# Gated delta-rule attention with two routed experts: value tiles turned through DRAM and in 32 x 32 blocks instead of by matmuls

## The chip, the cores and the metric

One Trainium2 chip, of which the kernel uses one core. The metric is the device time of one execution in microseconds (us), the median of several runs. Beside it stands one execution taken by the hardware profiler, with its own time.

## What is computed

A sequence of 2048 tokens with 512 features is normalised, and goes through two branches whose product is added to the input. The first branch is a recurrent attention with 16 value heads and 8 key heads (two value heads share a key head); the second is a feed-forward layer with the two experts that the router picks.

```python
xn = layernorm(x)
q, k, v = split(silu(causal_conv(xn @ W_qkv)))     # 8 + 8 + 16 heads of 128
q, k = l2norm(q) * 128 ** -0.5, l2norm(k)          # each repeated for two value heads
beta, g = sigmoid(xn @ W_b), -exp(A_log) * softplus(xn @ W_a + dt_bias)
def step(S, (q, k, v, g, beta)):                   # for each token and value head
    S = S * exp(g)
    S = S + outer(k, (v - k @ S) * beta)
    return S, q @ S
o = scan(step)
s = (o * rsqrt(mean(o * o) + eps) * norm_weight * silu(xn @ W_z)) @ W_out
y = x + s * silu(experts(xn))                      # two of eight experts
```

## The kernel before

The recurrence is computed by chunks of 128 tokens. A block is 512 tokens (4 chunks, `CPS`) of one key head with its two value heads (`REP`); there are 32 blocks (`NU`), four to a key head. All engines have their programs written by hand, one function each (`tensor` for PE, `scalar` for ACT, `vector` for DVE, `gpsimd` for POOL, `sync` for the DMA queue of SP), and each engine runs its instructions in the order in which they are written. They wait for each other by counting semaphores (`S_`). In each of these functions `attention_step(st)` is called for st = 2 to 34 at the most, and works on up to four blocks at once: it projects and convolves block st (`now`) and parts of block st + 1 (`ahead`), prepares block st - 1 (`turned`) and runs the chain of the recurrence over block st - 2 (`chain`).

A value tile goes this way. PE projects 512 tokens of one value head (`project` with kind v0 or v1) into a PSUM bank, ACT multiplies it by the first tap (`tap`), DVE adds the other three (`convolve`, three instructions of 128 x 512), and ACT writes the SiLU into `vS`, with features on the partitions and tokens along them. The chain needs tokens on the partitions. So `turn_v(st, half)` on PE turns two chunks of two heads by four matmuls with the identity, into a PSUM bank; it is called twice a step, behind `chain_out(st - 2, 1)` and behind `chain_out(st - 2, 2)`. `put_v(st, half)` on ACT then copies the turned tiles to `v_tok`, each token multiplied by the length of its key (`roots`). `chain_R` on DVE reads `v_tok` one step later.

Each of the four links i of the chain is: `chain_keys` (PE, keys and queries times the state S; waits for S), `chain_R` (DVE), `chain_solve` (PE), `chain_U` (ACT, copies U out of PSUM), `chain_state` and `chain_out` (PE, both read U), `chain_S` (DVE, the new S). PE fills the time between the links with projections. At the end of a step stand on PE `chain_state(3)`, `chain_out(3)`, `pair_matrices`, `join_y64`, then in the next step `chain_keys(0)` and `turn_q`; on DVE `chain_S(3)`, in each fourth block a clearing of S (`zero_state`), and `convolve(st, "v0")`. `turn_q` writes the bank from which `convolve(st, "v0")` reads, and so waits for its last instruction:

```python
def turn_q(st):
    ...
        pe.wait_ge(S_["conv_v0"], CONV * b)
```

A second loop runs beside the chain: small triangular inverses. 32 x 32 pieces of `CP` go to DRAM (`a_dram`), come back spread over the partitions (`A_in`), POOL eliminates, the result goes to DRAM (`v_dram`) and comes back into `VT`; DVE turns its diagonal blocks (`diagonal`, line 1400), and PE joins them (`join_y32`, line 511). The queue of SP also fetches decays (`E`, `decb`) and weights (`w_raw`), in the order of its program. After the attention come the experts (`up`, `down`), during which the results are turned by way of `og_x` and `og_y` (DVE, 32 x 32 blocks), and the output projection.

Of the kernel before, what the change touches and what calls it, by code (L numbers as in the profile page):

```python
# [6 lines left out]
P = 128  # L7
T, D = 2048, 512
KEY_HEADS, HEADS, HD = 8, 16, 128
KW = 4  # L10
# [65 lines left out]
rows_out eg0 eg1 dec0 dec1 begin0 begin1 a_out a_in v_out vt_in  # L76
xT smallT ab_turned sums score_parts scores_sum rows_turned
proj_k proj_q proj_v0 proj_v1 z_proj k_turned q_turned v_turned pair_kq keys queries solved state_add out_add lev_y32 lev_z32 lev_y64 lev_z64
sw_hi xn_hi ab_T ab_in exp_steps exp_sum rows
tap_k tap_q tap_v0 tap_v1 act_k act_q act_v0 act_v1 carry_k carry_q carry_v0 carry_v1 z_gate q_sq k_rem v_tok U squares y32 z32 y64 inv w_hi  # L80
softplus_steps router_steps stats var shift xn xn_lo beta softplus router rows_zero
conv_k conv_q conv_v0 conv_v1 nk nk_eps nk_beta c_neg c_rem q_eps CP E V_diag S_zero R S ms og w_lo_kq
# [8 lines left out]
def build(nc, x, small_w, group_w, conv_w, dt_bias, a_log, norm_w, w_out, w1, b1, w2, b2, const, where, og_dram, out):  # L91
# [5 lines left out]
    with top:  # L97
# [9 lines left out]
        ogT_dram = nc.dram_tensor("ogT_dram", (NT, P, HEADS, P), f32, kind="Internal").ap()  # L107
        v_dram = nc.dram_tensor("v_dram", (2, NPROB, B32, B32), f32, kind="Internal").ap()
# [28 lines left out]
        vS = alloc(att, "vS", [REP, SB])  # L137
# [54 lines left out]
        v_tok = alloc(p2b, "v_tok", [2, CPS, REP * HD])  # L192
# [57 lines left out]
        TQ_BANK, TK_BANK, TV_BANK = WORK_B, WORK_C, (WORK_C, WORK_B)  # L250
# [65 lines left out]
        CONV = 3  # L316
        SOLVES = B32 - 1
# [21 lines left out]
        def tensor(pe):  # L339
# [79 lines left out]
            def project_v0(st):  # L419
                if is_block(st - 1):  # L420
                    pe.wait_ge(S_["v_tok"], 2 * st)
                else:
                    pe.wait_ge(S_["conv_k"], CONV * 2)
                project(st, "v0")
# [57 lines left out]
            def turn_k(st):  # L482
                b = st - 1
                pe.wait_ge(S_["v_tok"], 2 * b + 1)
# [3 lines left out]

            def turn_v(st, half):
                b = st - 1  # L490
                pe.wait_ge(S_["act_v0"], b + 1)
                pe.wait_ge(S_["act_v1"], b + 1)
                if half:
                    pe.wait_ge(S_["z_gate"], CPS * b + 3)
                elif is_block(st):
                    pe.wait_ge(S_["CP"], CPS * (st + 1))
                elif b:
                    pe.wait_ge(S_["k_rem"], b)
                for i in range(2):
                    c = 2 * half + i  # L500
                    for h in range(REP):
                        r = pe.transpose(TV_BANK[half][:, (REP * i + h) * P:(REP * i + h + 1) * P], vS[:, h, c * P:(c + 1) * P], C["ident"])  # L502
# [1694 lines left out]
```

## Time and profile before

| | |
|---|---|
| median of 3 runs | 2063.14 us (2057.46 to 2063.60) |
| the profiled execution: its time | 2060.95 us |
| its span, first to last instruction | 2059.2 us |
| mean granted TensorE clock | 0.989 of full speed |
| busy: PE, DVE, ACT, POOL | 97%, 65%, 44%, 41% |
| attention, its steady steps | from about 140 to 1190 us |

The profile is of one execution. Busy is the time in which an engine executes, as a share of the span; it is a mean over stages with different limits. "Idle before" names the engine whose work ended last before an instruction could start. Matmuls overlap each other, so the distance between the starts of two groups tells better than their durations how long PE was taken. In the timeline a row can stand for several like instructions (x2, x4). PE, DVE, ACT, POOL are the engines; SPq and ACTq are DMA issues by SP and ACT.

### The profile page before, as it was taken

The numbers are of one execution on the slowest core, as the hardware profiler recorded it, in microseconds if no ns is written. First come the engines' busy times: TensorE is split into PE (matmuls) and PEld (weight loads), VectorE is DVE, ScalarE is ACT, GpSimd is POOL, SyncE is SP. The second block draws the span as 40 slices with busy tenths as digits, with TensorE's granted clock in tenths as the row PEclk, the third lists the DMA queues.
The fourth block names the chain that finished last, engine by engine and source line by source line (L and its number), as shares of the span: only waits on it lengthen the run. The fifth ranks groups of instructions, "written<-read, shape, count | busy, mean of one in ns | idle before, by whom it ended". The sixth has DMA issues, their size and how long they took to land.

```text
span 2059.2 us, 39550 instructions
## 1 busy us (share of the span) xinstructions
PE 1997.2 (97%) x13730; PEld 1705.4 (83%) x13730; DVE 1337.3 (65%) x3097; ACT 911.0 (44%) x2525; POOL 836.8 (41%) x2123
## 2 busy tenths in 40 slices
PE   5789999999999999999999999999999999999999
PEld 3578888888888888888888888888888888887887
DVE  6768887778787777887786445555555444447442
ACT  4465555555556565655554532222333233224221
POOL 2456576666666665757665411000111110111111
PEclk8899999999999999999999999999999999999999
DMA  4234444454336444444444223433334534303441
GB/s 131 47 74 81 102 87 96 82 94 83 93 84 106 82 98 92 86 92 84 97 80 85 84 82 72 92 78 76 83 80 84 123 82 103 72 21 123 154 149 66
DMA packets 388022, 184.25 MB, mean 89 GB/s; under 512 B 249456, under 2 KB 369136, under 8 KB 385776
## 3 DMA queue, kind: packets, MB, share of 16 engines
q1 hardware_dynamic: 354640, 177.73, 37.9%
q10 hardware_dynamic: 33184, 4.01, 1.3%
q8 instruction: 110, 1.80, 0.4%
q14 instruction: 88, 0.72, 0.1%
HBM read 135.26 MB, written 46.40 MB: 88 GB/s over the span
## 4 chain that ended last, share of the span: by engine, by line
PE 75%; issue 10%; DVE 6%; DMA 3%; POOL 3%; ACT 3%; SPq 1%; POOLq 0%; ACTq 0%; DVEq 0%
PE bank L333 18%; PE bank L335 18%; PE bank L334 18%; PE bank L565 3%; PE bank L574 2%; PE bank L548 2%; DMA VT<-v_dram 2%; PE bank L468 2%; PE bank L556 2%; PE bank L584 2%; PE bank L527 2%; PE bank L533 2%; POOL y_out L1825 1%; PE bank L502 1%; DVE cvx_k L1340 1%
## 5 line engine op out<-in xcount | busy, mean ns | idle before, releaser
L1771 POOL TENSOR_TENSOR prod<-A_in,V 128x60 f32<-128x60 f32 (+24 forms) x992 | 304.0, 306 | 270.6 <-DMA A_in<-a_dram 200.2
L1773 POOL TENSOR_TENSOR V<-V,prod 128x60 f32<-128x60 f32 (+24 forms) x992 | 311.6, 314 | 77.7
L1098 ACT ACTIVATE hid<-bank,bias 128x512 f32<-128x512 f32 x128 | 88.4, 691 | 455.0 <-PE bank L335 453.2
L1815 POOL TENSOR_TENSOR ffn_w_lo<-ffn_raw,ffn_w_hi 128x1024 fp32r<-128x1024 f32 x32 | 78.0, 2439 | 468.6 <-ACT ffn_w_hi L1088 464.7
L1563 DVE TENSOR_TENSOR h_lo<-hid,h_hi 128x512 fp32r<-128x512 f32 x128 | 91.1, 712 | 266.0 <-ACT h_hi L1105 266.0
L1577 DVE SCALAR_TENSOR_TENSOR gate_acc<-bank,rw,gate_acc 128x512 f32<-128x512 f32 x240 | 177.4, 749 | 58.8 <-PE bank L335 58.8
L333 PE MATMUL bank<-ffn_w_hi,h_hi 128*128 128x512 f32 x512 | 199.3, 389 | 1.3 <-DVE h_lo L1563 1.0
L333 PE MATMUL bank<-xn_hi,ffn_w_hi 128*128 128x512 f32 x512 | 200.3, 391 | 0.0
L335 PE MATMUL bank<-xn_hi,ffn_w_lo 128*128 128x512 f32 x512 | 199.3, 389 | 0.0
L334 PE MATMUL bank<-xn_lo,ffn_w_hi 128*128 128x512 f32 x512 | 199.2, 389 | 0.0
L334 PE MATMUL bank<-ffn_w_lo,h_hi 128*128 128x512 f32 x512 | 199.2, 389 | 0.0
L335 PE MATMUL bank<-ffn_w_hi,h_lo 128*128 128x512 f32 x512 | 199.2, 389 | 0.0
L1442 DVE SCALAR_TENSOR_TENSOR S<-S,total,bank 128x128 f32<-128x128 f32 x256 | 77.5, 344 | 139.9 <-PE bank L574 138.6
L333 PE MATMUL bank<-w_hi_z,xn_hi 128*128 128x256 f32 x512 | 154.1, 301 | 7.5 <-DVE cvx_v L1340 4.8
L1340 DVE SCALAR_TENSOR_TENSOR cvx_v<-bank,taps,cvx_v 128x512 f32<-128x512 f32 x192 | 143.0, 745 | 7.7 <-ACT cvx_v L874 3.1
L334 PE MATMUL bank<-w_lo_z,xn_hi 128*128 128x256 f32 x512 | 143.4, 280 | 0.0
L335 PE MATMUL bank<-w_hi_z,xn_lo 128*128 128x256 f32 x512 | 143.4, 280 | 0.0
L333 PEld LDWEIGHTS bank<-ffn_w_hi,h_hi 128*128 128x128 f32 x512 | 96.1, 188 | 21.8 <-issue 2.1
L335 PEld LDWEIGHTS bank<-ffn_w_hi,h_lo 128*128 128x128 f32 x512 | 96.2, 188 | 20.1
L334 PEld LDWEIGHTS bank<-xn_lo,ffn_w_hi 128*128 128x128 f32 x512 | 96.3, 188 | 19.5
L335 PEld LDWEIGHTS bank<-xn_hi,ffn_w_lo 128*128 128x128 f32 x512 | 96.0, 188 | 19.9
L333 PEld LDWEIGHTS bank<-xn_hi,ffn_w_hi 128*128 128x128 f32 x512 | 96.1, 188 | 19.7
(222 smaller groups left out, 5151.2 us busy)
## 6 DMA issues: line engine op xcount, KB each, us to landing
E<-eg_dram SPq DMA_DIRECT2D x64, 256.0 KB, 7.6
A_in<-a_dram SPq DMA_DIRECT2D x32, 512.0 KB, 4.0
decb<-dec_dram SPq DMA_DIRECT2D x128, 128.0 KB, 4.2
og_dram<-og SPq DMA_DIRECT2D x64, 256.0 KB, 2.2
ffn_raw<-w SPq DMA_DIRECT2D x32, 512.0 KB, 4.0
og_x<-og_dram SPq DMA_DIRECT2D x256, 64.0 KB, 2.6
ogT_dram<-og_y SPq DMA_DIRECT2D x64, 256.0 KB, 2.4
og_in<-ogT_dram SPq DMA_DIRECT2D x16, 1024.0 KB, 5.3
```

The costliest lines, as they stand in the source:

```text
L333: pe.matmul(ps, lh, rh, start=first, stop=False)
L334: pe.matmul(ps, lh, rl, start=False, stop=False)
L335: return pe.matmul(ps, ll, rh, start=False, stop=last)
L565: r = pe.matmul(bank[K_BANK][:, (REP + h) * HD:(REP + h + 1) * HD], VT[:, b % 2, REP * i + h, :], R[:, h, :], start=True, stop=True)
L1098: act.activation(hid[:, i % 2, :], bank[i % 4][:, :], ACT.Gelu_apprx_tanh, bias=bias1[:, k, f * NF + ft:f * NF + ft + 1]).then_inc(S_["gel ...
L1340: dve.scalar_tensor_tensor(cv[:, at], P_BANK[kind][:, :], taps[:, 4 * gr + n, j:j + 1], cv[:, at], MUL, ADD).then_inc(S_[f"conv_{kind}"], 1)
L1442: r = dve.scalar_tensor_tensor(S[:, h, :], S[:, h, :], total[:, cg, h0 + h:h0 + h + 1], bank[K_BANK][:, h * HD:(h + 1) * HD], MUL, ADD)
L1563: dve.tensor_tensor(h_lo[:, hb, ft, :], hid[:, i % 2, :], h_hi[:, hb, ft, :].bitcast(f32), SUB).then_inc(S_["h_lo"], 1)
L1577: dve.scalar_tensor_tensor(gate_acc[:, t, :], bank[4 + c][:, :], rw[:, k, t:t + 1], gate_acc[:, t, :], MUL, ADD).then_inc(S_["acc"], 1)
L1771: pool.tensor_tensor(prod[:, 0:m, 0:n], column, V[:, vb, 0:m, j:j + 1].to_broadcast([P, m, n]), MUL).then_inc(S_["product"], 1)
L1773: pool.tensor_tensor(V[:, vb, 0:m, j + 1:B32], V[:, vb, 0:m, j + 1:B32], prod[:, 0:m, 0:n], ADD).then_inc(S_["solve_step"], 1)
L1815: pool.tensor_tensor(fw[m, "lo", n % 2][:, :], raw[:, i % 2, :], fw[m, "hi", n % 2][:, :].bitcast(f32), SUB).then_inc(S_["ffn_lo"], 1)
```

## The change

The eight matmuls per block that turn the value tiles are gone from PE, with the PSUM banks that they used. In their place:

- `silu` writes the two heads side by side by chunks into `vS`, and `store_v` on ACT stores `vS` to DRAM (`vs_dram`) with one DMA of 512 KB, 128 rows of 4 KB, right behind `silu(v1)`, ahead of `chain_U(st - 2, 1)`.
- `load_v` on SP loads it back with four DMAs of 128 KB into `v_x`, in pieces of 32 values (128 bytes), behind the two decay loads in the second half of the step. After this load each 32 x 32 block is in the place where it has to be, but not yet turned.
- `turn_v` on DVE turns the blocks, in two instructions of 128 x 512 (two chunks of two heads each), behind `chain_S(st - 2, 3)` and ahead of `convolve(st, "v0")`, and writes `v_tok`, of which there is now one instead of two.
- `put_v` on ACT multiplies `v_tok` in place by the key lengths, both halves at the end of the step behind `put_y64`.
- Some waits follow: `project_v0` on PE waits for the third z gate instead of for `put_v`; `turn_k` takes over the wait that `turn_v` had; the four semaphores `carry_...` become one.

```diff
--- before
+++ after
...
@@ -105,6 +105,7 @@
         ogT_dram = nc.dram_tensor("ogT_dram", (NT, P, HEADS, P), f32, kind="Internal").ap()
+        vs_dram = nc.dram_tensor("vs_dram", (B32, NQD, REP * SB), f32, kind="Internal").ap()
         v_dram = nc.dram_tensor("v_dram", (2, NPROB, B32, B32), f32, kind="Internal").ap()
@@ -134,7 +135,7 @@
         q_sq = alloc(att, "q_sq", [4, CPS])
-        vS = alloc(att, "vS", [REP, SB])
+        vS = alloc(att, "vS", [CPS, REP, P])
         neg_inv = alloc(att, "neg_inv", [NT, HEADS])
@@ -189,7 +190,8 @@
         Y64 = alloc(p2b, "Y64", [NCH, 2 * B32])
-        v_tok = alloc(p2b, "v_tok", [2, CPS, REP * HD])
+        v_tok = alloc(p2b, "v_tok", [CPS, REP, HD])
+        v_x = alloc(p2b, "v_x", [NQD * REP * CPS, B32])
         z_gate = alloc(p2b, "z_gate", [2, CPS, REP * HD])
@@ -247,7 +249,7 @@
         KQ_BANK = (WORK_C, WORK_C)
-        TQ_BANK, TK_BANK, TV_BANK = WORK_B, WORK_C, (WORK_C, WORK_B)
+        TQ_BANK, TK_BANK = WORK_B, WORK_C
 
@@ -314,6 +316,7 @@
         CONV = 3
+        X_SET = 16 + 16 * NQD
         SOLVES = B32 - 1
@@ -418,7 +421,7 @@
                 if is_block(st - 1):
-                    pe.wait_ge(S_["v_tok"], 2 * st)
+                    pe.wait_ge(S_["z_gate"], CPS * (st - 1) + 3)
                 else:
@@ -481,26 +484,13 @@
                 b = st - 1
-                pe.wait_ge(S_["v_tok"], 2 * b + 1)
+                if is_block(st):
+                    pe.wait_ge(S_["CP"], CPS * (st + 1))
+                else:
+                    pe.wait_ge(S_["k_rem"], b)
                 for c in range(CPS):
                     i = pe.transpose(TK_BANK[:, c * P:(c + 1) * P], kqT[:, b % KQ_LIFE, c, 0, :], C["ident"])
                 i.then_inc(S_["k_turned"], 1)
-
-            def turn_v(st, half):
-                b = st - 1
-                pe.wait_ge(S_["act_v0"], b + 1)
-                pe.wait_ge(S_["act_v1"], b + 1)
-                if half:
-                    pe.wait_ge(S_["z_gate"], CPS * b + 3)
-                elif is_block(st):
-                    pe.wait_ge(S_["CP"], CPS * (st + 1))
-                elif b:
-                    pe.wait_ge(S_["k_rem"], b)
-                for i in range(2):
-                    c = 2 * half + i
-                    for h in range(REP):
-                        r = pe.transpose(TV_BANK[half][:, (REP * i + h) * P:(REP * i + h + 1) * P], vS[:, h, c * P:(c + 1) * P], C["ident"])
-                r.then_inc(S_["v_turned"], 1)
 
@@ -616,8 +606,6 @@
                     chain_out(st - 2, 1)
-                if turned:
-                    turn_v(st, 0)
 
@@ -631,7 +619,6 @@
                 if turned:
-                    turn_v(st, 1)
                     turn_k(st)
...
@@ -858,19 +841,23 @@
+            carries = 0
+                nonlocal carries
+                carries += 1
-                    act.copy(cv[:, 0:KW - 1], C["zero"][:, 0:KW - 1]).then_inc(S_[f"carry_{kind}"], 1)
+                    act.copy(cv[:, 0:KW - 1], C["zero"][:, 0:KW - 1]).then_inc(S_["carry"], 1)
-                    act.copy(cv[:, 0:KW - 1], cv[:, SB:SB + KW - 1]).then_inc(S_[f"carry_{kind}"], 1)
+                    act.copy(cv[:, 0:KW - 1], cv[:, SB:SB + KW - 1]).then_inc(S_["carry"], 1)
-                act.wait_ge(S_[f"carry_{kind}"], b + 1)
+                act.wait_ge(S_["carry"], carries)
@@ -886,8 +873,9 @@
                     if b:
-                        act.wait_ge(S_["v_turned"], 2 * b)
-                    dst = vS[:, int(kind[1]), :]
+                        act.wait_ge(S_["v_x"], X_SET * b)
+                    dst = vS[:, :, int(kind[1]), :]
+                    src = src.rearrange("p (c t) -> p c t", c=CPS)
                 act.activation(dst, src, ACT.Silu).then_inc(S_[f"act_{kind}"], 1)
@@ -923,12 +911,19 @@
                     act.wait_ge(S_["k_len"], b + 1)
-                if b >= 2:
-                    act.wait_ge(S_["R"], CPS * (b - 1))
                 for i in range(2):
                     c = 2 * half + i
-                    r = act.mul(v_tok[:, b % 2, c, :], TV_BANK[half][:, i * REP * HD:(i + 1) * REP * HD], roots[:, b % 4, c:c + 1])
+                    r = act.mul(v_tok[:, c, :, :], v_tok[:, c, :, :], roots[:, b % 4, c:c + 1])
                 r.then_inc(S_["v_tok"], 1)
+
+            def store_v(b):
+                act.wait_ge(S_["act_v0"], b + 1)
+                act.wait_ge(S_["act_v1"], b + 1)
+                if b:
+                    act.wait_ge(S_["v_turned"], 2 * b)
+                else:
+                    act.wait_ge(S_["xT"], 14)
+                act.dma_start(vs_dram.rearrange("i b t -> b i t"), vS[:, :, :, :].rearrange("p c h t -> p (c h t)")).then_inc(S_["v_x"], 16)
 
@@ -1020,6 +1015,7 @@
                     silu(st - 1, "v1")
+                    store_v(st - 1)
                 if chain:
@@ -1030,8 +1026,6 @@
                     mean_squares(st - 2, 1)
-                if turned:
-                    put_v(st, 0)
 
@@ -1044,7 +1038,6 @@
                 if turned:
-                    put_v(st, 1)
                     put_k(st)
@@ -1073,6 +1066,8 @@
                     put_y64(st - 1)
+                    put_v(st, 0)
+                    put_v(st, 1)
 
...
@@ -1400,6 +1396,15 @@
 
+            def turn_v(b):
+                dve.wait_ge(S_["v_x"], X_SET * (b + 1))
+                if b:
+                    dve.wait_ge(S_["R"], CPS * b)
+                for half in range(2):
+                    src = v_x[:, :, :].rearrange("p (b c h) j -> p c h b j", b=NQD, h=REP)[:, 2 * half:2 * half + 2, :, :, :].rearrange("p c h b j -> p (c h) b j")
+                    dst = v_tok[:, 2 * half:2 * half + 2, :, :].rearrange("p c h (b j) -> p (c h) b j", b=NQD)
+                    dve.transpose(dst, src).then_inc(S_["v_turned"], 1)
+
             def split_weights(n):
@@ -1417,7 +1422,7 @@
                     r = dve.scalar_tensor_tensor(R[:, h, :], bank[K_BANK][:, h * HD:(h + 1) * HD], decay[:, cg, h0 + h:h0 + h + 1],
-                                                 v_tok[:, b % 2, i, h * HD:(h + 1) * HD], MUL, SUB)
+                                                 v_tok[:, i, h, :], MUL, SUB)
                 r.then_inc(S_["R"], 1)
@@ -1547,6 +1552,8 @@
                     chain_S(st - 2, 3)
+                if turned:
+                    turn_v(st - 1)
                 if now:
...
@@ -1926,6 +1934,13 @@
 
+            def load_v(b):
+                sp.wait_ge(S_["v_x"], X_SET * b + 16)
+                for q in range(NQD):
+                    r = slice(q * B32, (q + 1) * B32)
+                    src = vs_dram.rearrange("i b (m t) -> i (b m) t", t=P)[:, :, r]
+                    sp.dma_start(v_x[r, :, :], src).then_inc(S_["v_x"], 16)
+
             def store(p):
@@ -1971,6 +1986,8 @@
                 next_decay(3)
+                if turned:
+                    load_v(st - 1)
                 if now and st % NSB == 1 and group + 1 < KEY_HEADS:
...
```

The order of instructions on three engines, at one place each; names are those of tiles, L is the line in the kernel's own file, x2 a count of like instructions.

On DVE, from the end of a step that clears no state, over its last state update into the next step, before:

```order
L1466 SCALAR_TENSOR_TENSOR og<-bank,roots,z_gate 128x128 x4
L1344 SCALAR_TENSOR_TENSOR E<-E,cst 128x256 x2
L1442 SCALAR_TENSOR_TENSOR S<-S,total,bank 128x128 x2
L1340 SCALAR_TENSOR_TENSOR cvx_v<-bank,taps,cvx_v 128x512 x3
L1363 SCALAR_TENSOR_TENSOR CP,norms<-bank,cst 128x128 x2
```

and after the change:

```order
L1471 SCALAR_TENSOR_TENSOR og<-bank,roots,z_gate 128x128 x4
L1340 SCALAR_TENSOR_TENSOR E<-E,cst 128x256 x2
L1447 SCALAR_TENSOR_TENSOR S<-S,total,bank 128x128 x2
L1406 STREAM_TRANSPOSE v_tok<-v_x 128x512 x2
L1336 SCALAR_TENSOR_TENSOR cvx_v<-bank,taps,cvx_v 128x512 x3
L1359 SCALAR_TENSOR_TENSOR CP,norms<-bank,cst 128x128 x2
```

Two transposes have come between the state update and the convolution whose end `turn_q` waits for.

On PE, behind the second link of the chain (state, out, then keys of the third link), before:

```order
L335 MATMUL bank<-w_hi_z,xn_lo 128x256
L574 MATMUL bank<-U,k_rem 128x128 x2
L584 MATMUL bank<-U,CP 128x128 x2
L502 MATMUL bank<-cst,vS 128x128 x4
L548 MATMUL bank<-S,kqT 128x256
L556 MATMUL bank<-S,qd 128x128 x2
```

and after the change:

```order
L338 MATMUL bank<-w_hi_z,xn_lo 128x256
L564 MATMUL bank<-U,k_rem 128x128 x2
L574 MATMUL bank<-U,CP 128x128 x2
L538 MATMUL bank<-S,kqT 128x256
L546 MATMUL bank<-S,qd 128x128 x2
```

The keys of the third link now stand directly behind the second link's output.

On ACT, in the first half of a step, before:

```order
L984 DMA a_dram<-CP 32x8x32 x2
L991 DMA v_dram<-V 256x1x32 x2
L891 ACTIVATE vS<-cvx_v 128x512
L962 COPY U<-bank 128x256
L871 COPY cvx_k<-cvx_k 128x3
```

and after the change:

```order
L979 DMA a_dram<-CP 32x8x32 x2
L986 DMA v_dram<-V 256x1x32 x2
L879 ACTIVATE vS<-cvx_v 128x4x128
L926 DMA vs_dram<-vS 4x32x1024
L957 COPY U<-bank 128x256
L858 COPY cvx_k<-cvx_k 128x3
```

The store has come between the SiLU of head 1 and the copy of U for which `chain_state(1)` waits.

## Rows read from the trace of the kernel before

**Rows 1.** Busy us (count) of PE, PEld, DVE, ACT, POOL, clock, DMA share, GB/s

```profile
600.00:900.00 300.00, 299.15 (x2693) 265.41 (x2692) 238.56 (x656) 171.44 (x577) 195.38 (x570) 1.00 0.46 93
```

**Rows 2.** Timeline of PE, links 2 and 3 of one step: start, duration

```profile
620.28 0.60 PE L502 MATMUL bank<-cst,vS 128*128 128x128 f32 x4
620.72 0.68 PE L548 MATMUL bank<-S,kqT 128*128 128x256 f32 x2
...
627.58 0.60 PE L502 MATMUL bank<-cst,vS 128*128 128x128 f32 x4
628.01 0.60 PE L486 MATMUL bank<-cst,kqT 128*128 128x128 f32 x4
628.45 0.60 PE L548 MATMUL bank<-S,kqT 128*128 128x256 f32 x2
```

**Rows 3.** Timeline of DVE, the state updates 1, 2 and 3 of that step

```profile
620.03 0.61 DVE L1442 SCALAR_TENSOR_TENSOR S<-S,total,bank 128x128 f32<-128x128 f32 x2 [1.95 <-PE bank L574]
...
627.33 0.61 DVE L1442 SCALAR_TENSOR_TENSOR S<-S,total,bank 128x128 f32<-128x128 f32 x2 [0.93 <-PE bank L574]
...
636.25 0.61 DVE L1442 SCALAR_TENSOR_TENSOR S<-S,total,bank 128x128 f32<-128x128 f32 x2 [1.54 <-PE bank L574]
```

**Rows 4.** Chain of waits over the end of a step that clears S

```profile
669.88 0.61 DVE S L1442 x2
...
672.54 0.76 DVE cvx_v L1340
673.30 0.14 issue
673.44 0.63 PE bank L479 x4
```

**Rows 5.** Timeline of DVE, end of a step that clears nothing

```profile
703.50 0.61 DVE L1442 SCALAR_TENSOR_TENSOR S<-S,total,bank 128x128 f32<-128x128 f32 x2 [0.23 <-PE bank L574]
704.02 2.32 DVE L1340 SCALAR_TENSOR_TENSOR cvx_v<-bank,taps,cvx_v 128x512 f32<-128x512 f32 x3
```

**Rows 6.** Timeline of PE there: `turn_q` of the next step

```profile
706.76 0.60 PE L479 MATMUL bank<-cst,kqT 128*128 128x128 f32 x4
```

**Rows 7.** Instructions on tile og_y: ns min/median/max, first and last start

```profile
L1604 DVE STREAM_TRANSPOSE og_y<-og_x x64: 668/702/707, 1246.5 to 1798.0; 128x512 f32<-128x512 f32 x64
```

**Rows 8.** Timeline of ACT, `chain_U(1)` of two steps

```profile
652.93 0.36 ACT L962 COPY U<-bank 128x256 f32<-128x256 f32 x1
...
686.04 0.36 ACT L962 COPY U<-bank 128x256 f32<-128x256 f32 x1
```

**Rows 9.** Timeline of PE, `chain_state(1)` of the same steps

```profile
653.34 0.71 PE L574 MATMUL bank<-U,k_rem 128*128 128x128 f32 x4
...
687.06 0.60 PE L574 MATMUL bank<-U,k_rem 128*128 128x128 f32 x4
```

**Rows 10.** Timeline of ACT, a `put_v`, and the wait of `put_z64`

```profile
607.47 0.58 ACT L955 COPY VT<-bank 64x512 f32<-64x512 f32 x1 [2.00 <-PE bank L533]
...
621.00 0.84 ACT L930 ACTIVATE v_tok<-bank,roots 128x256 f32<-128x256 f32 x2
```

**Rows 11.** DMA issues of the page: count, KB each, median us to landing

```profile
A_in<-a_dram SPq DMA_DIRECT2D x32, 512.0 KB, 4.0
...
og_x<-og_dram SPq DMA_DIRECT2D x256, 64.0 KB, 2.6
...
VT<-v_dram SPq DMA_DIRECT2D x128, 32.0 KB, 7.8
```

**Rows 12.** Timeline of SP: start and duration of issues

```profile
618.28 0.54 SPq L1911 DMA_DIRECT2D A_in<-a_dram  x1
...
625.46 2.81 SPq L1890 DMA_DIRECT2D decb<-dec_dram  x2
...
690.46 1.38 SPq L1890 DMA_DIRECT2D decb<-dec_dram  x2
```

**Rows 13.** Instructions on tile og_x: ns of an issue, min/median/max

```profile
L2019 SPq DMA_DIRECT2D og_x<-og_dram x256: 303/505/1757, 1194.5 to 1779.0; - x128
```

**Rows 14.** Tile VT, 300 to 1100 us: engines idle before its instructions (us, times)

```profile
  DMA VT<-v_dram: 10.4, 8
...
  DVE V L1400: 10.6, 9
  PEld bank L511: 8.8, 8
  PE bank L511: 5.5, 6
```

More of the change, by code:

```diff
@@ L75 @@
 ffn_bias ffn_bias1 ffn_raw0 ffn_raw1 wo_raw og_raw0 og_raw1 og_turned0 og_turned1 og_in0 og_in1 og_in2 x_res0 x_res1 out0 out1
-rows_out eg0 eg1 dec0 dec1 begin0 begin1 a_out a_in v_out vt_in
+rows_out eg0 eg1 dec0 dec1 begin0 begin1 a_out a_in v_out vt_in v_x
 xT smallT ab_turned sums score_parts scores_sum rows_turned
-proj_k proj_q proj_v0 proj_v1 z_proj k_turned q_turned v_turned pair_kq keys queries solved state_add out_add lev_y32 lev_z32 lev_y64 lev_z64
+proj_k proj_q proj_v0 proj_v1 z_proj k_turned q_turned pair_kq keys queries solved state_add out_add lev_y32 lev_z32 lev_y64 lev_z64
 sw_hi xn_hi ab_T ab_in exp_steps exp_sum rows
-tap_k tap_q tap_v0 tap_v1 act_k act_q act_v0 act_v1 carry_k carry_q carry_v0 carry_v1 z_gate q_sq k_rem v_tok U squares y32 z32 y64 inv w_hi
+tap_k tap_q tap_v0 tap_v1 act_k act_q act_v0 act_v1 carry z_gate q_sq k_rem v_tok U squares y32 z32 y64 inv w_hi
 softplus_steps router_steps stats var shift xn xn_lo beta softplus router rows_zero
-conv_k conv_q conv_v0 conv_v1 nk nk_eps nk_beta c_neg c_rem q_eps CP E V_diag S_zero R S ms og w_lo_kq
+conv_k conv_q conv_v0 conv_v1 nk nk_eps nk_beta c_neg c_rem q_eps CP E v_turned V_diag S_zero R S ms og w_lo_kq
 half_pow rstd sw_lo k_len qd factor product solve_step w_lo_vz
@@ L663, in up_part @@
                     pe.wait_ge(S_["z_gate"], CPS * NU)
-                elif k == 0 and i == 1:
-                    pe.wait_ge(S_["v_tok"], 2 * NU)
                 elif k == 0 and i == 2:
@@ L767, in tensor @@
             project_z(1, 1)
-            turn_v(1, 0)
             project_q(1)
             project_z(1, 2)
-            turn_v(1, 1)
             turn_k(1)
@@ L1190, in scalar @@
             silu(0, "v1")
+            store_v(0)
             put_z(1, 0)
@@ L1195, in scalar @@
             put_z(1, 1)
-            put_v(1, 0)
             exponents(3)
@@ L1200, in scalar @@
             put_z(1, 2)
-            put_v(1, 1)
             put_k(1)
@@ L1209, in scalar @@
             rates(3)
+            put_v(1, 0)
+            put_v(1, 1)
             for st in range(2, NU + 2):
@@ L1690, in vector @@
             gate_series(3)
+            turn_v(0)
             convolve(1, "v0")
@@ L2090, in sync @@
             load_blocks(1)
+            load_v(0)
             sp.wait_ge(S_["rows_out"], 96)
```

## The prediction

> **What bounds the kernel now.** I read first the busy times of a stretch in the middle of the attention: PE executes in 299.15 of 300 us, DVE in 238.56, ACT in 171.44, and the DMA engines are busy for 0.46 of the time, with the clock full [rows 1]. So a step of the attention is as long as PE needs, and two questions decide the change: which PE time really goes, and which new wait of PE comes. For this I looked at the timelines of PE and DVE side by side where the removed matmuls stand, then at the end of a step, where the new DVE work goes.
>
> The removed matmuls stand at two places. Four of them start at 620.28, and the keys of link 2 at 620.72; four more at 627.58, `turn_k` at 628.01, the keys of link 3 at 628.45 [rows 2]. A group of four thus takes 0.44 us of PE, and a block has two. The keys wait for the state, though, and the state is updated by DVE from 620.03 to 620.64 and from 627.33 to 627.94 [rows 3]. How long a wait on DVE takes to reach PE shows where PE did wait: the last convolution ends at 673.30, `turn_q` starts 0.14 later [rows 4].
>
> **The matmuls removed.** First place: the state is there at 620.64 + 0.14 = 620.78. The keys are on record from 620.72, but with 0.68 us where the undisturbed ones take 0.60 [rows 2]; their second matmul was already late by 0.08. In the three blocks after this one the row reads 0.68 too. So PE already waits here for the state, and without the transposes it waits 0.44 longer: gain 0. The bounds are 0 and 31 x 0.44 = 13.6 us (the loop turns 31 blocks). Second place: without the four, `turn_k` moves to 627.58 and the keys could start at 628.01, but the state allows 627.94 + 0.14 = 628.08. Gain 628.45 - 628.08 = 0.37, times 31 = **-11.5 us**. The work that gave PE something to do during the state update was useful cover, and half the gain is gone with it.
>
> **The transposes on DVE.** A DVE transpose of 128 x 512 takes 0.702 us [rows 7]. The next instruction starts about 0.09 before the recorded end of the one ahead (703.50 + 0.61 = 704.11, and the next starts at 704.02 [rows 5]), so two of them push back what follows by 2 x 0.702 - 2 x 0.09 = 1.22 us. What follows is the convolution of v0, and queued behind that are the key norms, `chain_R(0)` and the pairs of the next step. The first to wait is PE: `turn_q` needs the bank. The convolution ends at 704.02 + 2.32 = 706.34 [rows 5], is known on PE at 706.48, and `turn_q` starts at 706.76 [rows 6]: spare 0.28. So `turn_q` comes 1.22 - 0.28 = 0.94 late. Where the state is cleared there is no spare, PE waits already [rows 4], and the whole 1.22 is added. Of the 29 steps which have both a `turn_v` and a next `turn_q`, 7 clear the state: 22 x 0.94 + 7 x 1.22 = **+29.2 us**. Below it lies nothing if the convolution were somehow not the last to come; above it 29 x 1.40 = 41 if nothing overlaps. `chain_R(0)` and the pairs run later too, but PE has `join_z64` and a whole projection of v1 ahead of them, over 3 us, so they cost nothing of their own.
>
> Here the Trainium skill has another price. "VectorE: DVE Perf Modes", section "The three transpose paths", gives 311 ns on VectorE and 390 ns on TensorE for a bf16 tile of 128 x 128. An estimate by that page would make eight tiles 2.5 us on DVE for 3.1 us on PE. The rows of this trace are for f32 and several tiles an instruction: 0.18 us a tile on DVE and 0.11 on PE, both lower, and PE the cheaper. By the page this term would be about +66 us and the gain of the removed matmuls larger; the sum goes by the rows.
>
> **The store on ACT.** It stands ahead of `chain_U(1)`. An issue of the same form, 128 rows of 4 KB, takes SP 0.54 us [rows 12], and I take that for ACT. U is copied from 652.93 on and `chain_state(1)` starts at 653.34, 0.41 after the start of the copy; a step later it is 686.04 and 687.06, 1.02 [rows 8, 9]. In the first kind PE comes for U at once, in the second there are 0.61 to spare. Of five blocks that I looked at two are of the first kind; I take half of 31: 15 x 0.54 = **+8 us**, bounds 0 and 31 x 0.54 = 17. Behind it a later U makes a later state, and the keys of link 2 wait for that.
>
> **What the store does to the other transfers.** The store begins just behind the load of `A_in` [rows 12], at about the time of `E`, and `VT` follows. A transfer of 512 KB lands after 4.0 us and one of 64 KB after 2.6 [rows 11]: so 512 KB hold the engines for about 1.4 us. `VT` takes 7.8 to land [rows 11], and is late already: DVE waits for it 8 times in 800 us (24 blocks), 10.4 us in all, and PE 14 times for DVE's blocks, 14.3 us [rows 14]. If `VT` lands 1.4 later, the third of the blocks with no spare loses that: 10 x 1.4 = 14 us. But in blocks where U or `turn_q` is late the need is later as well; I take half, rounded down, **+6 us**; bounds 0 and 31 x 1.4 = 43.
>
> The Trainium skill speaks against the change at this point. "DMA: Bandwidth & Descriptors", section "Issuing engines are not separate DMA queues", says that transfers issued by different engines run on the same 16 DMA engines and interleave. By this rule the store on ACT's queue does hold up `VT` on SP's; if queues were separate, this term would be 0.
>
> **The load.** It is in 128-byte pieces, as is `og_x`. It moves 512 KB, as eight loads of `og_x` do: issuing them takes 8 x 0.505 = 4.0 us [rows 13] and the last lands 2.6 later [rows 11], 6.7 in all. It can begin behind the second `decb` issue, at 690.46 + 1.38 = 691.84, and is there at 698.5; DVE comes for it at 704.02 [rows 5]. In steps that fetch z weights the issue ends at 625.46 + 2.81 = 628.27 [rows 12]: there at 635.0, wanted at 636.25 + 0.52 = 636.8 [rows 3]. So it is hidden, **0**, by the twelve or eight us of the second half of the step. If it takes as long to land as `VT`, 7.8 instead of 2.6, it is there at 640.1, 3.3 late in every fourth block: +26 us, the other bound. Queued behind it on SP are the result store and two decay loads of the next step, which have a whole link of time.
>
> **put_v at the end.** `put_v` costs 0.84 per half [rows 10], 1.7 both. At the end of the step ACT has 2.00 us of idle time before `put_z64` [rows 10], and `put_z64` waits for matmuls behind `turn_q`, which come later than now. So 0; if that cover went, the U of link 0 would be later by up to 1.7, which `project_v1` on PE still hides. The relief of ACT in the middle of the step is worth nothing, since PE waits for ACT there only through U. The start of the program loses two groups of matmuls and gains two transposes: 0 within 2 us.
>
> **The sum.** -11.5 + 29.2 + 8 + 6 = +31.7 us on the profiled execution's 2060.95 gives 2092.7. That execution lies 2.2 below the median of the runs, 2063.14, so the forecast is **2095 us**. A measurement here tells about 0.3%, 6 us, from no change.
>
> **The rivals.** (a) My forecast, slower by a wait of PE at `turn_q`: chance 0.70. Its own range is 2070 to 2125: without the two terms of the store and with two thirds of the wait it is 2095 - 14 - 10 = 2071; with U late in every block (+9) and half of the upper end for `VT` (+21) it is 2125.
>
> (b) Faster. The mechanism is at `turn_q`: if the convolution is not what it waits for in most steps, or two transposes in a row delay it by less than 0.28, the gain of the second place stays and nothing is paid: 2063 - 11.5 = 2052; with the first place too, 2038. It decides for faster from the point where `turn_q`'s added wait is under 0.4 us a block. The wait of PE in the steps that clear the state [rows 4] speaks against it; for it, that PE is the bound and gets less work. Chance 0.13.
>
> (c) No change. The waits at `turn_q` are half of what I work out, since later stalls elsewhere (the 14.3 us at `join_y32`) shrink when the step gets longer: -11.5 + 15 + 0 = 2067. Chance 0.07.
>
> (d) The load is late in every block. DVE then waits ahead of the convolution, with everything behind it: each us costs 30. It needs a landing more than 12 us after the `decb` issue. Against it stand the rows of `og_x`, for it that the queue holds `VT` and decays ahead of it. 2 us late: 2095 + 60 = 2155. Chance 0.10. The skill's page on DMA, section "Why small descriptors are slow (HBM only)", names a fixed cost for each packet, which would favour (d); no row here shows it as more than `og_x` has.
>
> The range is 2062 to 2125: it leaves out most of (b) and (d). Slower by over 0.3% are (a) and (d) and a little less for the lower edge of (a), 0.79; within 0.3% 0.08; faster 0.13.
>
> **What would show it.** In the profile after: keys of link 2 with PE idle or a matmul stretched by 0.4 us behind `chain_out(1)`, released by the state update; `turn_q` released by the convolution of v0 in nearly all blocks, about 1 us each; the transposes at 0.70 us with no DMA wait before them; the state of link 1 waiting for U in half the blocks; DVE's wait for `VT` up from 10.4 us. The prediction is wrong if `turn_q` does not wait, or if DVE waits for `v_x`.

## The result, and the profile after

The changed kernel takes 2159.28 us (median of 4 runs, 2155.74 to 2167.13) against 2062.51 of the kernel before: ratio 1.048, 95% interval 1.0457 to 1.0503, so 97 us slower where I forecast 32 and a range of -1 to +62. The profiled execution has 2156.11 us, a span of 2154.3 and a mean granted clock of 0.974 (before 0.989). The loss lies in the attention: the first copy of U starts at 130.9 us and the last at 1282.3, 1151.4 between them, where before it was 131.9 to 1187.1, 1055.2.

The busy times of the stretch that [rows 1] shows for before:

```profile
600.00:900.00 300.00, 281.64 (x2477) 243.27 (x2476) 230.18 (x620) 160.11 (x528) 178.98 (x527) 0.97 0.55 113
```

PE executes 281.64 of 300 us instead of 299.15 and gets 2477 matmuls done instead of 2693 (the removed ones are eight of a block, some 70 in such a stretch). DVE, ACT and POOL are less busy too; the DMA engines are at 0.55 instead of 0.46. PE waits for somebody, and part of the time it has the lower clock. The waits of PE, DVE and SP between 300 and 1100 us (us in total, times, longest):

```profile
PE bank L482 <- DVE cvx_v L1336: 23.6, 21, 3.2
PE bank L501 <- DVE V L1396: 16.9, 13, 3.2
PE bank L538 <- DVE S L1447: 7.6, 23, 1.4
PE bank L564 <- ACT U L957: 2.5, 4, 0.8
...
DVE V L1396 <- DMA VT<-v_dram: 23.0, 16, 3.6
DVE E L1340 <- DMA E<-eg_dram: 7.0, 4, 3.4
DVE v_tok L1406 <- DMA v_x<-vs_dram: 4.3, 4, 2.1
...
SPq L1942 <- DMA vs_dram<-vS: 66.9, 19, 6.8
```

The first, third and fourth rows are the waits that the prediction named: `turn_q` for the convolution, the keys for the state, `chain_state` for U. But `join_y32` (L501) has gone from 5.5 to 16.9 us and DVE's wait for `VT` from 10.4 to 23.0 [rows 14], and SP stands 66.9 us for the store to land. The transposes themselves take a little less than forecast, 0.670 us, and the load is hardly waited for (tile v_x):

```profile
L1942 SPq DMA_DIRECT2D v_x<-vs_dram x128: 591/666/3253, 108.6 to 1253.0; - x128
L1406 DVE STREAM_TRANSPOSE v_tok<-v_x x64: 653/670/712, 115.6 to 1261.0; 128x512 f32<-128x512 f32 x64
```

One step shows what the store does. First ACT and then SP and DVE in the same stretch:

```profile
622.32 0.63 ACT L879 ACTIVATE vS<-cvx_v 128x512 f32<-128x512 f32 x1 [3.50 <-DVE cvx_v L1336]
623.02 0.58 ACTq L926 DMA_DIRECT2D vs_dram<-vS  x1
623.70 0.37 ACT L957 COPY U<-bank 128x256 f32<-128x256 f32 x1 [0.75 <-ACT vS L879]
```

```profile
622.43 1.10 SPq L1890 DMA_DIRECT2D E<-eg_dram  x2
623.63 3.21 SPq L1935 DMA_DIRECT2D VT<-v_dram  x4
626.89 3.30 SPq L1898 DMA_DIRECT2D decb<-dec_dram  x2
636.59 2.94 SPq L1942 DMA_DIRECT2D v_x<-vs_dram  x4
...
637.18 1.33 DVE L1396 STREAM_TRANSPOSE V<-VT 32x256 f32<-32x256 f32 x3 [2.58 <-DMA VT<-v_dram]
```

U is copied behind the issue of the store, and waited for it: the solve on PE that U comes from has ended at 622.49. `VT` is issued at 623.63, and DVE idles 2.58 us for it, until 637.18. SP comes to the load only at 636.59, 13 us behind the end of the store's issue. The chain of waits over this place puts it in two lines:

```profile
625.77 11.39 DMA VT<-v_dram
638.07 0.45 DVE V L1396
```

### The profile page after: what moved, and what is told of

Same layout as the page of the kernel before. It is cut to its first block, busy times and chain, and to the rows that moved or that the text cites. A ratio compares the mean times of both kernels' runs of the same rounds, so it can differ in the third digit from the quotient of the medians.

```text
span 2154.3 us, 39261 instructions
## 1 busy us (share of the span) xinstructions
PE 2018.5 (94%) x13474; PEld 1704.5 (79%) x13474; DVE 1376.6 (64%) x3161; ACT 917.3 (43%) x2525; POOL 832.6 (39%) x2123
## 4 chain that ended last, share of the span: by engine, by line
PE 49%; DMA 14%; DVE 12%; issue 11%; SPq 6%; POOL 5%; ACT 1%; ACTq 1%; DVEq 0%; POOLq 0%
PE bank L336 13%; PE bank L337 13%; PE bank L338 13%; DMA VT<-v_dram 7%; DVE cvx_v L1336 3%; SPq L1935 2%; PE bank L555 2%; DMA E<-eg_dram 2%; DVE v_tok L1406 2%; POOL V L1781 2%; POOL prod L1779 2%; DVE CP L1383 1%; DMA a_dram<-CP 1%; PE bank L564 1%; DVE S L1447 1%
## 5 line engine op out<-in xcount | busy, mean ns | idle before, releaser
L336 PE MATMUL bank<-w_hi_z,xn_hi 128*128 128x256 f32 x512 | 158.8, 310 | 7.8 <-DVE cvx_v L1336 4.8
L336 PE MATMUL bank<-xn_hi,w_hi_v 128*128 128x512 f32 x256 | 110.6, 432 | 3.8 <-DVE cvx_k L1336 2.2
L336 PEld LDWEIGHTS bank<-xn_hi,ffn_w_hi 128*128 128x128 f32 x512 | 96.5, 188 | 19.5
```

The source lines that it names most:

```text
L336: pe.matmul(ps, lh, rh, start=first, stop=False)
```

## The experiments

Differences below are between medians; each median is uncertain by some 2 to 5 us, so a difference of 6 us between two runs is not clear of noise. For the links of the chain I give the mean distance between the starts of the copies of U, over blocks 2 to 29 of each trace (link 0 is from U(0) to U(1)). A line number shifts by a few between kernels.

| kernel | us | ratio (95%) | link 0, 1, 2, 3 (us) |
|---|---|---|---|
| before | 2062.5 | 1 | 7.74, 6.67, 8.42, 10.97 |
| b1: before without matmuls | 2054.0 | 0.9960 (0.9943 to 0.9978) | 7.71, 6.66, 8.21, 11.02 |
| n2: transposes, no transfers | 2088.9 | 1.0142 (1.0104 to 1.0181) | 7.79, 6.63, 8.32, 12.17 |
| s4: n2 + tiny store | 2100.7 | 1.0194 (1.0168 to 1.0220) | 8.72, 6.29, 8.11, 12.01 |
| s2: n2 + store, contiguous rows | 2107.0 | 1.0224 (1.0199 to 1.0248) | 8.44, 6.28, 8.49, 12.03 |
| s1: n2 + store as changed | 2153.2 | 1.0456 (1.0435 to 1.0477) | 8.69, 6.29, 9.41, 12.26 |
| after | 2159.3 | 1.0480 (1.0457 to 1.0503) | 8.55, 6.29, 8.97, 12.75 |
| l1: n2 + loads | 2096.0 | 1.0163 (1.0144 to 1.0181) | 7.78, 6.66, 8.26, 12.11 |
| e1: after, contiguous store | 2113.5 | 1.0254 (1.0231 to 1.0276) | 8.31, 6.29, 8.45, 12.62 |

**The four edits of the full kernel.** They came first.

```diff
 e1   -act.dma_start(vs_dram.rearrange("i b t -> b i t"), ...)
      +act.dma_start(vs_dram.rearrange("i b t -> (i b) t"), ...)   # value columns of the weights permuted to match
 e2   turn_v(st - 1) from ahead of convolve(st, "v0") to behind it
 e3   store_v(st - 1) from ahead of chain_U(st - 2, 1) to behind it
 e4   e1, e2 and e3 together
```

> The change with the store's DRAM rows in the order of the partitions (the value features are permuted in the weights and taps so that the load needs no other change). Theory A (the store runs on few DMA engines, 25 rows of 4 KB per us, and holds up VT there): the store lands within about 4 us, DVE's wait for VT over 300 to 1100 us falls from 23.0 us to about 10, SP's wait for the store from 66.9 to under 15, and the time by 20 to 45 us, to 2115 to 2140. Theory B (the load's 4096 small pieces or the bytes as such are the contention): the shape of the store does not matter, 2150 to 2165.

> The change with the two DVE transposes behind the convolution of v0 instead of ahead of it. Theory A (the prediction's term of +29 us at turn_q is real, and some more is lost through the lower clock that follows): PE's wait at turn_q (23.6 us in 800) falls to near 0, the time to 2115 to 2135. Theory B (PE's waits at turn_q only take the place of waits that come later anyway): under 10 us gained, 2150 or more.

> The change with the store issued behind the copy of U of link 1 instead of ahead of it. Theory A (the store costs what ACT's issue costs, 0.6 us in most blocks): PE's wait for U in 300 to 1100 us (7.6 us of weight loads, 21 times) goes to about 0, the time falls by 8 to 20 us, to 2140 to 2150. Theory B (U is not on the path): no change, 2155 to 2162.

> Store spread, transposes behind the convolution, store behind U, all three. Theory A: the terms add and the clock comes back to 1.00, so that the time is at or below that of before: 2040 to 2075. Theory B (the transfers as such cost 40 us and more): 2090 or more.

e1 2113.49 us, 46 less than the changed kernel by nothing but the order of the store's rows, a little more than theory A gave. DVE's wait for `VT` is 10.5 us and SP's for the store 14.8, as theory A had it; the store lands after a median of 7.0 us, not 4. e2 2131.79 (1.0351, 1.0328 to 1.0375), 27 less, theory A: PE no longer waits at `turn_q`, but for U in its place (21.1 us in 22 waits between 300 and 1100 us). e3 2167.80 (1.0515, 1.0485 to 1.0544), 9 more, above both theories, though its interval overlaps that of the changed kernel: links 0 and 1 are back at 7.70 and 6.67, so U is in time, and links 2 and 3 rise to 9.74 and 12.99, since `VT` now comes still later (DVE waits 39.6 us for it instead of 23.0). e4 2096.83 (1.0169, 1.0143 to 1.0196), still 34 above before, theory B.

**Single parts against their absence.**

```diff
 n1   after without the two dve.transpose; put_v scales v_x
 n2   after without store_v and load_v; dve.transpose(v_tok, vS)
 b0   before without the eight pe.transpose; put_v scales vS
 e5   e1 and e2, store_v issued by SP behind load_inverse
```

> The change without the two DVE transposes: ACT scales the loaded tiles as they lie, so the value blocks stay unturned; store and load are as in the change. Theory A (turn_q's wait is the transposes' alone, about 1 us a block, and the clock loss hangs on the waits): PE's wait at turn_q near 0, time 2115 to 2135, VT still late. Theory B (the transfers alone make all of the loss): 2145 or more.

> The change without store and load: DVE turns the blocks straight out of vS, so the blocks are turned but stay in their old places. Theory A (removed matmuls -11, transposes +29, the rest of the +97 is transfers and clock): 2075 to 2092, VT waited for as before. Theory B (DVE's transposes and ACT's late scaling are most of it): 2110 or more.

> The kernel before with the matmuls that turn the value tiles left out and nothing in their place (ACT scales the unturned tiles). Theory A (the first place's gain is lost to the wait for the state): 11 us gained, 2046 to 2053. Theory B (both places gain, 0.88 us a block): 27 us gained, 2030 to 2037.

> Store spread over the engines and issued by SP behind the load of VT instead of by ACT, transposes behind the convolution. Theory A (what is left of the loss is the store ahead of E and VT on the DMA engines): DVE's waits for E and VT go back to those of before (12 and 10 us in 800), U is no longer late, time 2045 to 2070. Theory B (the transfers cost as such, or the load now comes too late): 2085 or more, with DVE waiting for v_x in the second case.

n1 2115.18 (1.0258, 1.0228 to 1.0287): 44 less than the changed kernel, theory A. n2 2088.93, theory A. b0 2059.79 (1.0001, 0.9984 to 1.0017), in neither range: the matmuls seemed to be worth nothing, but in b0 `project_v0` and `turn_k` still waited for `put_v`, which the change had undone too. e5 2081.78 (1.0095, 1.0064 to 1.0125), between its two ranges, is the best full version, and still 19 us above the kernel before.

**The sum taken apart.** The next four close the gap in b0 and separate store from load.

```diff
 b1   b0, and the waits of project_v0 and turn_k as in the changed kernel
 s1   n2 with store_v; silu waits for its landing
 l1   n2 with load_v in each step, store only once
 n4   n2 with turn_v(st - 1) behind convolve(st, "v0")
```

> The kernel before without the eight matmuls that turn the value tiles (put_v scales vS unturned, so the values are not turned), and with project_v0 waiting for the third z gate and turn_k for CP, as in the changed kernel; the run without the matmuls that came before this one kept both waiting for put_v. Theory A (the prediction's second place: 0.37 us of 31 blocks are really free): about 2051 us, ratio 0.995. Theory B (the matmuls lay under waits for the state, and nothing is gained at either place): 2059 to 2062, ratio 0.999 to 1.000.

> The changed kernel without the load: ScalarE stores as before the issue of U, 4 x 32 rows, and the next SiLU waits for its landing, but VectorE turns out of vS, so no transfer stands in its way (the 32 x 32 blocks come from the wrong quarters, and the last block isn't stored). Next to the kernel with neither transfer (2088.9): if the store's shape and place carry the loss (theory A), 2135 to 2150, with VectorE waiting for VT over 15 us in 300 to 1100 us; if the bytes alone do (theory B, store and load alike), about 2105 to 2115.

> The changed kernel with only one store, ahead of the steps, and with all the loads at their place on SyncE's queue, each free to start when the block's SiLU is done; what they bring is not used: VectorE turns out of vS. Theory A (the load is nearly free, the store costs): 2090 to 2098. Theory B (the load's 4096 pieces of 128 bytes hold up VT and E): 2105 or more.

> The changed kernel without store and load (VectorE turns out of vS, from the wrong quarters), and with the two transposes behind the convolution of v0 instead of ahead of it. If the wait of turn_q is the whole cost of the transposes (theory A): the 27 us that the kernel with neither transfer loses come back, 2055 to 2064. If the 1.2 us of VectorE only move to the next wait, the keys of link 0 or 1 or U (theory B): 2070 to 2085.

b1 2054.01, nearest to theory A: the matmuls are worth 8 us. s1 2153.20, more than theory A gave: the store alone carries 64 of the 97 us. l1 2095.96, theory A: the load costs 7, which is not clear of noise. n4 2074.28 (1.0058, 1.0038 to 1.0077): 15 of the 35 us of the transposes go with the wait of `turn_q`, 20 stay and stand in link 0 (8.56 instead of 7.71, of which link 1 gives back 0.40); theory B.

**Why the store costs 64, and a place for the transposes.**

```diff
 s2   s1 with the contiguous store of e1
 s4   s1, store of [:, :, 0:8] only (32 bytes a partition)
 m1   n2 with turn_v(st - 1) ahead of chain_S(st - 2, 3)
 c1   e5 with turn_v(st - 1) ahead of chain_S(st - 2, 3)
```

> The store-only kernel (2153.2 us; no load, VectorE turns out of vS, and the wrong blocks, last block not stored) with the store's rows contiguous, so that its outermost dimension is 128 instead of 4. Theory A (the shape holds the store on few DMA engines, VT is late for them): the third link goes back from 9.4 to 8.4 us a block, 2105 to 2115 us, the first link stays at 8.7. Theory B (any 512 KB at that moment make VT late): 2140 or more.

> The store-only kernel with 32 bytes a partition stored instead of 4 KB, same place ahead of the copy of U, same shape (4 x 32 rows). What is left of the store is its issue on ScalarE. Theory A (the prediction's term: the issue of 0.56 us delays U(1)): 2089 + 8 to 17 = 2097 to 2106, with the first and second link together 14.8 to 15.0 us a block instead of 14.4. Theory B (the issue costs nothing): 2086 to 2092.

> The changed kernel without store and load (VectorE turns out of vS, from the wrong quarters), with the two transposes ahead of the last state update, where VectorE waits 1.3 to 1.6 us for the matmul of the state, instead of behind it. If 1.2 us of VectorE cost only where they stand ahead of what is waited for: 2052 to 2060, near the kernel without any turning (2054). If VectorE's 1.2 us come back at another wait anyway, as they did behind the convolution: 2070 to 2080.

> A full version: contiguous store issued by SyncE behind the load of VT (as in the run of 2081.8 us), the load where it is, and the transposes ahead of the last state update. If the place of the transposes is worth here what it is without transfers: 2058 to 2068. If the load isn't there 1.2 us earlier, in steps with weight loads above all, VectorE waits for v_x ahead of the state update, which PE waits for: 2080 to 2110.

s2 2107.03 and s4 2100.66, theory A both times: of the store's 64 us its issue ahead of U is 12, its bytes 6 (not clear of noise), its shape 46. (In the 46 is a little of the issue: with contiguous rows it takes ACT 0.35 us instead of 0.57, at most 31 x 0.22 = 7 us; link 0 is 8.44 in s2 and 8.69 in s1.) The page's DMA part for the 13 us from the store's issue on (one digit for each fortieth, the busy share of 16 DMA engines in tenths) shows the shape. First s2:

```profile
DMA  9494998857765796552526657788661000000000
GB/s 101 164 214 151 353 397 303 258 129 195 208 202 227 303 359 274 211 202 98 57 32 96 96 120 228 196 171 177 209 192 50 3 6 13 6 0 0 0 0 0
DMA packets 2201, 1.95 MB, mean 150 GB/s; under 512 B 1184, under 2 KB 1952, under 8 KB 2200
```

and s1, with the same transfers:

```profile
DMA  9789984347779599779999979989523332222222
GB/s 202 227 302 416 397 268 107 88 82 79 88 82 66 47 88 79 60 41 101 102 109 140 210 212 223 240 268 329 186 107 110 113 113 104 104 91 91 90 66 70
DMA packets 2150, 1.92 MB, mean 147 GB/s; under 512 B 1166, under 2 KB 1901, under 8 KB 2149
```

s2 has moved its 1.95 MB after three quarters of the stretch and is idle. In s1 the same work drags on to the end with 0.2 to 0.3 of the engines busy, at 66 to 113 GB/s. The packets in the trace say whose it is: the store's 4 KB packets take 159 ns each in both, and go at 24 to 25 a us in s1, which is 24.5 x 0.159 = 3.9 engines' worth, and at 34 to 58 a us in s2. The ceiling holds in every block: between 140 and 1180 us no us of any store in s1 has more than 28 of its packets, where in s2 there are up to 97; the last packet starts a median of 11.1 us behind the issue in s1 and 6.5 in s2. `VT` consists of 1024 pieces of 128 bytes. In the block shown, 107 of them go in s1 only in the us in which the store ends, and the last one starts 13.2 us behind the store's issue; in s2 it starts after 9.7. `VT` is late by that: PE's wait at `join_y32` between 300 and 1100 us is 21.6 us in 14 waits in s1 and 7.0 in 7 in s2, and DVE's:

```profile
DVE V L1398 <- DMA VT<-v_dram: 28.7, 17, 3.7
```

```profile
DVE V L1398 <- DMA VT<-v_dram: 11.4, 11, 3.4
```

(s1 first). The decays are not what is late: DVE waits 11.2 us for `E` in s1 and 17.6 in s2. The issues of `VT` on SP take longer as well, again s1 first:

```profile
L1938 SPq DMA_DIRECT2D VT<-v_dram x84: 320/760/2398, 328.1 to 1071.6; - x84
```

```profile
L1938 SPq DMA_DIRECT2D VT<-v_dram x88: 321/580/1592, 321.7 to 1065.0; - x88
```

From the first copy of U to the last, s1 takes 43.9 us more than s2. In this time PE is idle for 92.1 us in s1 and 64.2 in s2, 28 more, of which `join_y32` has 19 (29.1 and 9.7). The rest goes with the clock: 34.1 us at the lower of its two levels against 6.8, and at half the clock that is at most 27.3 / 2 = 14 us lost.

m1 2069.43 (1.0035, 1.0021 to 1.0050), between my two cases: 15 of 35 us stay. In most steps the transposes are now hidden in the idle time ahead of the state update: link 3 grows over b1 by 1.3 in seven blocks (0, 4, ... 24), and by 0.23 or less, on average, in each other kind of step. In those seven DVE splits the next weights (`split_weights`) right ahead of the transposes and has no idle time left; 6 of the 9 waits at `turn_q` between 300 and 1100 us are there. c1 was to be the version that beats both kernels, and is a miss: 2150.69 (1.0444, 1.0411 to 1.0478), 69 worse than e5 and above both of my readings. DVE's waits ahead of the transposes and SP's for the store (us in total, times, longest):

```profile
DVE v_tok L1395 <- DMA v_x<-vs_dram: 36.1, 21, 4.3
...
SPq L1940 <- DMA vs_dram<-vS: 102.1, 22, 7.5
```

SP's wait is no longer than in e5, where it is 108.3 us; the first row is what is new. The load is wanted about 3 us earlier than in e5 (by the state update and the convolution), where DVE waits for it 2.7 us between 300 and 1100 us; it is not there, and the state, which PE waits for, is now queued behind it: link 3 is 14.36. Over the whole attention DVE waits 53.1 us for it in 29 blocks. From the first copy of U to the last PE is idle for 76.3 us (40.5 in e5), and 99 us are spent at the lower clock (17 in e5).

**The clock.** PE's mean granted clock between 300 and 1100 us is 1.00 before, 0.97 after, 0.95 in c1. The last two runs give PE its eight matmuls per block back as idle work.

```diff
 f1b  after + 2 x 4 pe.transpose(bank, kqT, ident) at the two old places of turn_v
 f2b  c1 + the same
```

> The changed kernel (2159.3 us) plus eight matmuls of 128 x 128 per block on TensorE at the two old places (two groups of four behind the second and the third link's output), that turn keys into banks which nobody reads: the old work of TensorE back as mere cover. Theory A (only the time of PE counts: the second place costs 8 us as in the kernel before, the clock does not answer to so small a piece): 2160 to 2170. Theory B (stretches at the lower clock come from PE's stalls, and less idle time in the step brings back part of the 75 us that are spent at the lower level): 2130 to 2152, with fewer than 50 us at the lower level.

> The full version with SyncE's contiguous store and the transposes ahead of the last state update (2150.7 us, with 99 us at the lower clock, the most of all runs) plus the same eight idle matmuls per block. Theory A (the time is set by the late load, the clock is only a result): 2150 to 2162. Theory B (the lower clock is a cost of its own and filler lessens it): 2120 to 2144, under 65 us at the lower level.

f1b 2168.32 us (1.0496, 1.0471 to 1.0520), not faster than the changed kernel; its profile has the clock at 0.99 in that stretch, and 58 us of the attention at the lower level instead of 75. That is one execution: over all of them the mean granted clock of the whole kernel is 0.977 in both. f2b 2172.14 (1.0511, 1.0482 to 1.0541), 21 us slower than c1, with 0.94 and 140 us at the lower level for c1's 99. f1b is in theory A's range, f2b above it. That filler helps, as theory B had it, is refuted by both times: idle matmuls here neither keep the clock up nor save time. What the lower clock itself costs these two didn't test, since they did not raise it.

## Why the prediction was right or wrong

The parts make a chain from before to after, each difference between two neighbours of the table: matmuls 2054.0 - 2062.2 = -8; transposes 2088.9 - 2054.0 = +35; the store's issue +12, its bytes +6, its shape +46; the load 2159.3 - 2153.2 = +6. That is 97. (2062.2 is the kernel before on the chip of b1.) Of the 65 us between my +32 and this, 46 stand in what the store does to the other transfers. The parts aren't strictly independent: taken out of the changed kernel the shape gives 46 and the transposes 44.

- **Matmuls removed, -11.5.** Right in kind, -8 measured (-4.5 to -12 by the interval of the ratio). In b1 link 2 is shorter by 0.21 and links 0 and 1 by 0.04 together, as forecast: the second place pays and the first does not. It took b1 to see it.
- **Transposes, +29.2.** The mechanism is right: in n2 `turn_q` waits for the convolution 23 times between 300 and 1100 us, in every block, 19.5 us in all. Against b1, link 3 grows by 0.95 (mean of 1.03, 0.98 and 0.85 for the three kinds of step that clear nothing, blocks 2 to 28) where I had 0.94. In the seven steps that clear the state it grows by 1.89 on average, with a median of 1.26, where I had 1.22, and links 0 and 2 grow with it. The three of them that take over 13 us have one or two stretches of 3.4 us at the lower clock, which my sum had no term for; in the other four it is 12.3. Measured 35; within my upper bound of 41. In this 35 are also `put_v` at the end of the step and the single `v_tok`.
- **The store's issue, +8 (0 to 17).** Measured 12: links 0 and 1 together are 15.01 in s4 and 14.42 in n2, 0.59 a block times 31 = 18, of which part is made up for in links 2 and 3.
- **What the store does to the other transfers, +6 (0 to 43).** This is the step that failed. I read 1.4 us of engine time for 512 KB out of [rows 11], the difference between `A_in` and `og_x`, and applied it to a transfer of another shape. It measured 6 for the bytes, which is my value, but by luck, since 6 us is within the noise of two runs; and 46 more for the shape, together 52, above my bound of 43. The late `VT` itself was forecast; what I had wrong is for how long a store of this shape holds it up. The store's pattern in DRAM is 4 x 32 rows, and its packets go at the rate of four of 16 engines. The Trainium skill has this rule, and I overlooked it: "DMA: Bandwidth & Descriptors", section "Why a DMA increments its semaphore by 16 and not by 1", says that the number of engines of a transfer is the largest up to 16 that divides the slowest dimensions of both patterns, so four here, and 16 for rows in one run of 128. The trace agrees, with 3.9 engines' worth, and e1, which changes only the order of the rows, gives the 46 us back. That `VT`'s late pieces lie behind the store's on the same four engines is inferred from when they go; no view names the engine of a packet. In the block shown, 790 of the 1024 pieces go in the store's first 3 us, and 234 later; four of 16 engines would have 256.
- **The load, 0 (to +26).** 6 to 7 measured, not clear of noise; DVE waits for it 4 times. It wasn't as quick as I thought (in e1 a part lands after a median of 5.6 us, not 2.6), and was hidden all the same. c1 shows how narrow that is.
- **put_v at the end, 0.** No run tests it alone. m1 has it, together with the transposes, at 15 us over b1, and where the transposes are hidden its link 3, which ends at the U of link 0, is as in b1. PE's wait for U comes from the store's issue, and is gone in e3.
- **Rivals.** (b) fell at n2: `turn_q` does wait. (c) had the terms shrink when the step gets longer; they added. (d), the late load, isn't what happened in the changed kernel, though its time, 2155, is near; it is what happened in c1.
- **Also in the sum of waits before.** The 14.3 us that I gave for PE at `join_y32` added the rows of matmul and weight load, which see the same waits; it is 5.5 to 8.8 (the two are partly one wait).

What stays open: in m1 the seven steps with `split_weights` hold 9 of the 15 us that remain (in one of them the clock is at its lower level), and 5 lie ahead of the first copy of U (132.5 us, 127.5 in b1), which is not traced to a cause. And whether the time at the lower clock is a cost of its own, or stands where PE would have waited anyway, is not shown: from s2 to s1 it is at most 14 of the 46 us, and in the changed kernel, with 75 us at the lower level, at most 75 / 2 = 38 of the 97.

## What to carry to other kernels

Look at the access pattern of a transfer before its bytes: with an outermost dimension of 4 the 32 stores of 512 KB cost 46 us more per execution than the same stores in 128 contiguous rows, for the most part through the loads beside them. A price read from one transfer holds only for one of its shape. And work put on VectorE, with a third of its time idle, still cost 15 to 35 us at three different places, since it stood in front of something that PE wanted; ask at each place what is queued behind, and for a load, how much earlier it is now wanted.

## What the runs showed of the hardware

- A store of 4 x 32 rows of 4 KB ran at the rate of four DMA engines, some 100 GB/s (24.5 x 4 KB a us); its issue on ACT took 0.57 us, that of the contiguous form 0.35. Issues of other loads on SP behind it took 0.76 us instead of 0.45 (medians for `VT`, s1 and n2; 0.58 in s2, with the contiguous store).
- A load of 128 KB in pieces of 128 bytes (a fourth of `v_x`) landed after a median of 5.6 us in e1, and took 0.67 us to issue in the changed kernel.
- From the first copy of U to the last, the granted clock was at the lower level of 1.2 GHz for 75 us in the changed kernel, in which PE was idle for 86.0 us, and for 3.4 us in the one before, with 16.9 us idle. The four matmuls of `turn_q` take 0.60 us in [rows 6], and in this row of the changed kernel's timeline 1.09, behind a wait of 1.80; the clock is at the lower level from 682.5 to 689.4:

```profile
682.74 1.09 PE L482 MATMUL bank<-cst,kqT 128*128 128x128 f32 x4 [1.80 <-DVE cvx_v L1336]
```
